# Both SiLUs of a Mamba-2 mixer by ScalarE's own Silu function instead of Tanh and a VectorE product, with the exponentials in the other function table

## The reference, cut to what matters

```
proj = hidden_states @ in_proj_w.T
gate, xBC, dt = jnp.split(proj, [INTER, INTER + CONV_DIM], axis=-1)
conv = causal depthwise convolution of xBC, 4 taps, + conv_b
xBC = jax.nn.silu(conv)                      # first SiLU
x, Bm, Cm = jnp.split(xBC, ...)
y = _ssd(x, Bm, Cm, D, dt, dt_bias)          # scores * exp(decay), two chunks of 128
yg = y * jax.nn.silu(gate)                   # second SiLU
rstd = rsqrt(mean(square(yg)) + EPS) for each of 8 groups
out = (yg * rstd) * norm_w @ out_proj_w.T
```

## Time and profile before

| | |
|---|---|
| median of 3 runs | 1625.1 us (1624.51 to 1627.74) |
| the profiled execution's own time | 1627.01 us |
| its span in the trace | 1625.2 us |
| TensorE busy | 1564.3 us, 96% |
| VectorE busy | 1228.0 us, 76% |
| GpSimd busy | 1052.0 us, 65% |
| ScalarE busy | 1002.3 us, 62% |
| one full mixer group (16 steps and the tail) | 182.5 us |

### The profile page before, as it was taken

One profiled execution on the slowest core, in us unless ns is written; L12 is line 12 of the kernel. 1 busy time (PEld: TensorE's weight loads), 2 busy tenths in 40 slices (PEclk: granted clock), 3 DMA queues, 4 the chain that ended last, 5 costly groups with the idle time before them and its releaser, 6 DMA issues. The chain is left out here.

```text
span 1625.2 us, 25474 instructions
## 1 busy us (share of the span) xinstructions
PE 1564.3 (96%) x8296; PEld 1226.0 (75%) x8296; DVE 1228.0 (76%) x1689; ACT 1002.3 (62%) x2122; POOL 1052.0 (65%) x790
## 2 busy tenths in 40 slices
PE   6979999999999999999999999999999999999979
PEld 4657777777777777777777777777777777777757
DVE  6688877787778877887688877887688877887565
ACT  4357765666666665666666665666666665666431
POOL 2017874788757874788657874787657874787620
PEclk9899999999999999999999999999999999999989
DMA  3033321323222221222212321223222221322011
GB/s 118 1 103 103 107 91 59 92 91 92 78 72 92 92 92 59 91 92 92 78 72 92 92 91 59 92 92 92 78 75 88 92 92 59 98 86 84 20 40 53
DMA packets 73658, 131.65 MB, mean 81 GB/s; under 512 B 10944, under 2 KB 10944, under 8 KB 73280
## 3 DMA queue, kind: packets, MB, share of 16 engines
q1 hardware_dynamic: 73536, 130.09, 24.3%
HBM read 127.44 MB, written 2.62 MB: 80 GB/s over the span
## 5 line engine op out<-in xcount | busy, mean ns | idle before, releaser
L892 DVE SCALAR_TENSOR_TENSOR mx_acc<-bank,mx_cw,mx_acc 128x510 f32<-128x510 f32 (+2 forms) x480 | 358.3, 746 | 160.8 <-ACT mx_acc L877 149.5
L159 PE MATMUL bank<-h_hi,mx_w_hi 128*128 128x512 f32 x1152 | 465.6, 404 | 4.4 <-DVE mx_acc L892 2.3
L161 PE MATMUL bank<-h_hi,mx_w_lo 128*128 128x512 f32 x1152 | 453.1, 393 | 0.0
L160 PE MATMUL bank<-h_lo,mx_w_hi 128*128 128x512 f32 x1152 | 450.2, 391 | 0.0
L1108 ACT ACTIVATE mx_mix<-mx_csb,mx_gncs 128x256 f32<-128x256 f32 x512 | 218.9, 499 | 284.3 <-PE bank L1478 281.3
L1033 POOL TENSOR_TENSOR mx_y<-mx_y,mx_sg 128x512 f32<-128x512 f32 x128 | 338.4, 2644 | 59.7 <-DVE mx_y L1280 51.7
L839 POOL TENSOR_TENSOR mx_w_lo<-mx_w_raw,mx_w_hi 128x512 fp32r<-128x512 f32 x144 | 187.4, 1302 | 111.0 <-ACT mx_w_hi L834 111.0
L161 PEld LDWEIGHTS bank<-h_hi,mx_w_lo 128*128 128x128 f32 x1152 | 216.9, 188 | 48.5
L159 PEld LDWEIGHTS bank<-h_hi,mx_w_hi 128*128 128x128 f32 x1152 | 217.3, 189 | 47.8 <-issue 6.5
L160 PEld LDWEIGHTS bank<-h_lo,mx_w_hi 128*128 128x128 f32 x1152 | 217.7, 189 | 41.5
L1262 DVE TENSOR_TENSOR mx_mix<-mx_mix,mx_cbt 128x1536 f32<-128x1536 f32 x128 | 224.5, 1754 | 0.0
(11 more groups left out here) (163 smaller groups left out, 2203.7 us busy)
## 6 DMA issues: line engine op xcount, KB each, us to landing
mx_csb<-cs_rows SPq DMA_DIRECT2D x128, 512.0 KB, 4.0
mx_w_raw<-in_w_in SPq DMA_DIRECT2D x144, 256.0 KB, 4.0
mx_wo_raw<-in_w_out SPq DMA_DIRECT2D x64, 256.0 KB, 4.2
res<-in_x SPq DMA_DIRECT2D x8, 256.0 KB, 5.0
f_base_raw<-in_base_wt SPq DMA_DIRECT2D x2, 1024.0 KB, 6.1
out<-res SPq DMA_DIRECT2D x8, 256.0 KB, 2.0
f_a_raw<-in_lora_a SPq DMA_DIRECT2D x2, 256.0 KB, 3.8
f_lb_raw<-in_lora_b SPq DMA_DIRECT2D x2, 256.0 KB, 6.2
```

The costliest lines, as they stand in the source:

```text
L159: nc.tensor.matmul(out, w_hi, x_hi, start=first, stop=False)
L160: nc.tensor.matmul(out, w_hi, x_lo, start=False, stop=False)
L161: return nc.tensor.matmul(out, w_lo, x_hi, start=False, stop=last)
L892: self.nc.vector.scalar_tensor_tensor(dst, src[:, :, 0:SEQ - k], self.cw[:, c, TAPS - 1 - k:TAPS - k], dst, ALU.mult, ALU.add).then_inc(s[ ...
```

## The change

ScalarE's `Silu` takes the place of Tanh and of the VectorE product, for the gate (from PSUM into `sg`) and for the convolution (in place in `acc`). VectorE's `silu_gate` and `silu_conv` go, with the buffer `th`. The semaphores `conv` and `sg`, which TensorE and GpSimd wait for, are now raised by ScalarE. The factors 0.5 in the small constant tables become copies. In the step, `square` and `round_tile` move from before `decay_from_second` to the step's end, so that the Exps stand together and everything between the first Silu and the next step's first Exp can use Silu's table.

```
-            def tanh_conv(g, u):
+            def silu_conv(g, u):
                 act.wait_ge(s["tap"], 1 + (TAPS - 1) * (UNITS * g + u + 1))
-                act.wait_ge(s["conv"], 1 + UNITS * g + max(u - 1, 0))
-                nc.scalar.activation(th[:, u % 2, :], acc[:, u % 4, :, :].rearrange("p b t -> p (b t)"),
-                                     ACT.Tanh).then_inc(s["th"], 1)
+                a = acc[:, u % 4, :, :].rearrange("p b t -> p (b t)")
+                nc.scalar.activation(a, a, ACT.Silu).then_inc(s["conv"], 1)
...
-            def tanh_gate(g, st):
+            def silu_gate(g, st):
                 act.wait_ge(s["gate"], 1 + STEPS * g + st + 1)
                 act.wait_ge(s["yg"], 1 + STEPS * g + max(st - 1, 0))
-                nc.scalar.activation(sg[:, st % 2, :], G_BANK[:, :], ACT.Tanh, scale=0.5).then_inc(s["tg"], 1)
+                nc.scalar.activation(sg[:, st % 2, :], G_BANK[:, :], ACT.Silu).then_inc(s["sg"], 1)
...
                     if here or more:
                         evacuate(gn, un)
+                    if here or more:
+                        decay_from_second(gn, stn)
+                    silu_gate(g, st)
+                    if here or more:
+                        silu_conv(gn, un)
+                    if st % 2 == 0:
+                        split_wo(g, st // 2)
+                    if here and has_tile(g, st + 1):
+                        round_tile(g, st + 1)
                     if st >= 1:
                         square(g, st - 1)
-                    if here and has_tile(g, st + 1):
-                        round_tile(g, st + 1)
-                    if here or more:
-                        decay_from_second(gn, stn)
-                    tanh_gate(g, st)
-                    if here or more:
-                        tanh_conv(gn, un)
-                    if st % 2 == 0:
-                        split_wo(g, st // 2)
...
-            def silu_conv(g, u):
-
-                dve.wait_ge(s["th"], 1 + UNITS * g + u + 1)
-                a = acc[:, u % 4, :, :].rearrange("p b t -> p (b t)")
-                nc.vector.scalar_tensor_tensor(a, th[:, u % 2, :], 1.0, a, ALU.add, ALU.mult).then_inc(s["conv"], 1)
...
-            def silu_gate(g, st):
-                dve.wait_ge(s["tg"], 1 + STEPS * g + st + 1)
-                a = sg[:, st % 2, :]
-                nc.vector.scalar_tensor_tensor(a, a, 1.0, G_BANK[:, :], ALU.add, ALU.mult).then_inc(s["sg"], 1)
```

More of the change, by code:

```diff
@@ L801, in __init__ @@
             "const_in", "nw_in", "const", "proj", "gate", "xt", "y", "cb", "out", "ss",
-            "evac", "th", "tg", "decay", "sq", "yhi", "whi", "wohi", "gcopy", "root",
+            "evac", "decay", "sq", "yhi", "whi", "wohi", "gcopy", "root",
             "tap", "conv", "mix", "xd", "sg", "ysb", "cbt", "gsum", "outsb", "ms", "inv", "wolo",
@@ L860, in conv_constants @@
         dve.wait_ge(s["tap"], 1 + (TAPS - 1) * UNITS * g)
-        nc.vector.tensor_scalar(self.cw[:, :, :], self.cw_raw[:, :, :], 0.5, None, ALU.mult).then_inc(s["const"], 1)
-        nc.vector.tensor_scalar(self.cb[:, :], self.cb_raw[:, :], 0.5, None, ALU.mult).then_inc(s["const"], 1)
+        nc.vector.tensor_copy(self.cw[:, :, :], self.cw_raw[:, :, :]).then_inc(s["const"], 1)
+        nc.vector.tensor_copy(self.cb[:, :], self.cb_raw[:, :]).then_inc(s["const"], 1)
         dve.wait_ge(s["const"], 1 + 5 * g + 2)
@@ L919, in mixer_phase @@
         csb = sb("csb", [P, 2, 2, HALF])
-        th = sb("th", [P, 2, HALF])
         xd = sb("xd", [P, 2, HB * 2, 2, HD])
@@ L1079, in _ @@
         def _(act):
-            start_at_one(act, [s["th"], s["tg"], s["decay"], s["sq"], s["wohi"], s["gcopy"], s["root"]])
+            start_at_one(act, [s["conv"], s["sg"], s["decay"], s["sq"], s["wohi"], s["gcopy"], s["root"]])
             start_after_quad(act, [s["yhi"]])
@@ L1154, in _ @@
             act.wait_ge(s["const"], 1 + 3)
-            tanh_conv(0, 0)
-            tanh_conv(0, 1)
+            silu_conv(0, 0)
+            silu_conv(0, 1)
             evacuate(0, 2)
@@ L1159, in _ @@
             evacuate(0, 3)
-            tanh_conv(0, 2)
+            silu_conv(0, 2)
             decay_from_second(0, 0)
             ip.round_w(act, 0, 3)
-            tanh_conv(0, 3)
+            silu_conv(0, 3)
             evacuate(0, 4)
-            tanh_conv(0, 4)
+            silu_conv(0, 4)
             def steps(g, more):
@@ L1202, in tail @@
                     ip.round_w(act, g + 1, 2)
-                    tanh_conv(g + 1, 1)
+                    silu_conv(g + 1, 1)
                     evacuate(g + 1, 2)
                     evacuate(g + 1, 3)
-                    tanh_conv(g + 1, 2)
-                    tanh_conv(g + 1, 3)
+                    silu_conv(g + 1, 2)
+                    silu_conv(g + 1, 3)
                     evacuate(g + 1, 4)
                     ip.round_w(act, g + 1, 3)
-                    tanh_conv(g + 1, 4)
+                    silu_conv(g + 1, 4)
                     root(g)
@@ L1232, in _ @@
         def _(dve):
-            start_at_one(dve, [s["conv"], s["mix"], s["xd"], s["sg"], s["ysb"], s["cbt"],
+            start_at_one(dve, [s["mix"], s["xd"], s["ysb"], s["cbt"],
                                s["ms"], s["inv"], s["wolo"]])
@@ L1327, in head_constants @@
                 dve.wait_ge(s["ysb"], 1 + STEPS * g)
-                nc.vector.tensor_scalar(dh[:, :], d_raw[:, :], 0.5, None, ALU.mult).then_inc(s["const"], 1)
-                nc.vector.tensor_scalar(gdt[:, :, :], m.dtt[:, :, bass.ds(g * GH, GH)], 0.5, None,
-                                        ALU.mult).then_inc(s["const"], 1)
+                nc.vector.tensor_copy(dh[:, :], d_raw[:, :]).then_inc(s["const"], 1)
+                nc.vector.tensor_copy(gdt[:, :, :], m.dtt[:, :, bass.ds(g * GH, GH)]).then_inc(s["const"], 1)
                 dve.wait_ge(s["const"], 1 + 5 * g + 5)
@@ L1343, in _ @@
             keep_bc(0, 1)
-            silu_conv(0, 4)
             def steps(g, more):
@@ L1356, in steps @@
                         ip.taps(dve, gn, un)
-                    silu_gate(g, st)
-                    if here or more:
-                        silu_conv(gn, un)
                     if st % 2 == 1:
```

8 lines of the change are left out of this document (removed).

## The result

The changed kernel took 1806.7 us (median of 4 runs, 1799.7 to 1814.6), the kernel before 1626.1 (4 runs, 1624.5 to 1627.7). The ratio is 1.111, 95% interval 1.106 to 1.117. The forecast was 1709 us, and its range ended at 1760. So the sign was right and the size was half of what came. The profiled execution is the fastest of the four, with a span of 1797.9 us at a granted clock of 0.976; the other three have 1800.5, 1809.3 and 1812.8 us at 0.973, 0.966 and 0.964.

What follows compares the result with a forecast made beforehand. TensorE, busy 96%, was taken to bound the kernel before, a loop ScalarE, GpSimd, ScalarE after. Group 0's 13.4 plus 7 x 10.1 gave 84 us: 1711 for the profiled execution, 1709 for the median, range 1650 to 1760.

Steps and rivals of the forecast that it cites:

- What GpSimd meets in its new place: GpSimd's later `split_tile`, `sum_squares` and select fall beside VectorE's `make_mix` and stretch: 12.0 us late at step 14.
- the meeting: GpSimd's rows overlapping VectorE's `make_mix` after `y`; 0.9 of each overlap added for a tensor_tensor, half for the select.
- A shorter loop: Rival: the overlap with `make_mix` costs nothing, 3.4 us a group, about 10 in group 0, 1659 us; chance 0.16.
- the ring: Loop of ScalarE's `round_tile`, GpSimd's `split_tile`, `sum_squares` and select, ScalarE's next first Exp: average 10.58 and 11.08 against 10.30 us.
- Two loads a step: ScalarE's table loads, 251 in all: 1.31 us each, about 0.1 more for lost overlap, no drain.
- The Silus take Tanh's places: ScalarE's gate and convolution: Silu costed at Tanh's 0.58 and 0.62 us.
- The moved `round_tile`: ScalarE's `yhi` comes at D (first Exp's start) + 7.01 to 8.13, before 5.1; loop 10.27 to 11.39 us without contention.
- VectorE's two products go: Taking both products from VectorE gains nothing inside a group and 0.4 us for each group, at its beginning.
- Group 0: First group: 2.9 us late from prelude loads, 2.7 in steps 1 to 7, some 7.5 from step 8; together 13.4.
- TensorE busy near 91%: Expected profile after the change: TensorE's busy share near 91%, before 96%.
- Select alone 0.63: Expected profile after the change: GpSimd's select takes 0.63 us where it stands alone, before 1.09 beside VectorE's product.
- Transposes waiting about 1 us for Silu: Expected profile after the change: TensorE's transposes wait for ScalarE's Silu about 1 us a step, most from step 5.

Runs made afterwards that it cites:

- run 4: The changed kernel with `make_mix` reading its second operand from PSUM (another tile's data, so values differ), 1678.0 us.
- run 11: The changed kernel with GpSimd's first select ahead and the gate's Silu ahead of `decay_from_second`, so four table loads a step, 1924.7 us.
- Run 7: The changed kernel with Tanh for both Silus (no table loads in the steps, values differ) and `square` and `round_tile` back in their old place, 1609.4 us.
- runs 1 and 5: The changed kernel with `square` and `round_tile` back before the second Exps, 1645.5 us; the second also with GpSimd's first select ahead, 1644.8 us.
- run 3: The changed kernel with GpSimd's first select of the next but one step ahead of `split_tile` and `sum_squares`, 1628.6 us.
- run 5: The changed kernel with `square` and `round_tile` back before the second Exps and GpSimd's first select ahead of `split_tile` and `sum_squares`, 1644.8 us.

## Why the prediction was half right

The mechanism was the one forecast and the size was not. The step that failed is **"What GpSimd meets in its new place"**. The prediction made the meeting worth 50 us (1709 less the 1659 of "A shorter loop"); it measured 129 (1806.7 less the 1678.0 of run 4). I put `make_mix` 0.6 us behind `y` in all steps and walked 12.0 us of lateness to step 14. In step 2 it does start there (739.75, with `y` at 739.08). In step 3 it starts 1.9 us behind `y` (751.24, with `y` at 749.32): VectorE's queue is itself late, since its taps wait for `evacuate`, which comes only after the first Exp of the late ring. So VectorE stands inside the ring. In run 4, where nothing is stretched, `make_mix` starts about 0.7 us behind `y` again. I had seen that shift under "A shorter loop" and thought that it would shrink the overlap. It fixed it instead: steps 3 to 8 all take 11.9 or 12.1 us, where I had 10.9 to 12.3.

By stretches of the middle group of the table (203.2 us against 182.2; forecast 10 more, measured 21; the six between group 0 and the last average 22.2):
- D3 to D9: +10.2, forecast +6.5. The meeting is locked in.
- D0 to D3: +4.0, forecast none. I had said the ring binds only from step 3. But the first Exp waits for the select from step 1 on (0.71 us at 721.51, 1.83 at 732.17), and `split_tile` (2.80 us at 739.88) and the select (2.15 at 729.99) meet `make_mix` there too. Without the meeting (run 4) 1.1 of the 4.0 are left.
- D9 to D14: +6.5, forecast +5.5. Nearly right.
- D14 to D15: +2.8, forecast none. Here the code has one more wait, for the constants, ahead of the Exp. That Exp's own wait for the select then seems to go to its load, which doesn't start early and lies 0.07 us behind the select's end:

```profile
884.26 0.64 POOL L1020 TENSOR_SCALAR_AFFINE_SELECT mx_csb<-mx_csb 128x512 f32<-128x512 f32 x1
```
```profile
884.97 1.28 ACT L1106 ACT_TABLE_LOAD   x1 [3.14 <-issue]
886.26 1.71 ACT L1106 ACTIVATE mx_mix<-mx_csb,mx_gncs 128x256 f32<-128x256 f32 x4
```

- D15 to D0: -2.5, forecast -1.9 (1.8 of lateness that TensorE doesn't feel, and the ends). Near, but by luck: without the low clock it is -4.1 (group 6), with two spells of it -0.9 (groups 1 and 2).

The other steps:
- *Two loads a step.* 273 loads in the trace, before 22: 251. All take 1283 ns, with no drain, also in a full ScalarE (run 11). Right. The Trainium skill, "ScalarE: Activation LUTs", What ACT_TABLE_LOAD costs, gives 2.66 us for a switch, drain included; these traces disagree, with 1.28 us and 0.01 to 0.02 us to the next row.
- *The Silus take Tanh's places.* Gate 0.597 us, convolution 0.62. Right.
- *The moved `round_tile`.* The ring without the meeting was summed to 10.27, 10.89, 10.77 and 11.39 us. Run 4 shows it bare: 10.38, 10.87, 10.75 and 11.35. Right.
- *"A shorter loop"* priced a kernel without the meeting at 1659; run 4 measured 1678. That sum lacked group 0's size (14.0 us late at group 1's D0, where I had about 10) and the last step's load.
- *VectorE's two products go.* I gave it 0.4 us a group. Run 7 shows 16 us: 8.2 in group 0 (148.4 to 140.2), where VectorE paces the early steps, and 0.9 in each other group. The trace of before had the place (group 0's steps of 8 us), and I priced that place only for ScalarE.
- *Group 0.* Forecast 13.4, though its terms 2.9, 2.7 and 7.5 make 13.1; measured 19.4 at group 1's D0 (302.3 against 282.9).
- *TensorE busy near 91%*: 89%. *Select alone 0.63*: 0.64. *Transposes waiting about 1 us for Silu*: 0.53, 1.58 and 1.73 us in three steps in a row.
- *The clock.* The prediction has no term for it. The stretch from D15 to D0 takes 30.4 us in groups 1 and 2, with two spells of 3.4 us at 0.50 in it, 28.8 in groups 3 to 5 with one, and 27.2 in group 6 with none: 1.6 us for each. Steps late in groups 4 to 7 take 12.7 or 12.8 us instead of 11.4, and each follows such a spell. In group 4 it lies from 1025.5 to 1028.9, right behind 2.2 us of idle time of TensorE; `make_mix` starts 1.6 us later against the first Exp than in group 3 (8.0 us behind it, there 6.3) and meets `split_tile`, 2.71 us at 1038.30, where group 3 has 1.31 at 835.17. Together that is some 21 us of the 173 (an estimate, from the seven group ends and six late steps).

Reconciled: 84, 6 more in group 0, 12.1 more in each of six groups, 10.1 in the last, give 173, which is the difference of the two spans (1797.9 less 1625.2). The 181 us between the medians are 8 more, since the changed kernel's profiled execution is its fastest.

What stays open: the other 52 us of run 4 weren't split by a run of their own between ring, group 0, the late load and the clock. No run held the clock fixed, so what it took of the 129 us is known only from the traces. And why the same idle time is followed by a low clock in one group and not in the next isn't shown: in runs 1 and 5 one or two groups of seven were spared after the same 2.2 us.

## What to carry to other kernels

When an instruction is moved later in one engine's queue, follow what stands behind its receiver in the receiver's queue. Here a rounding moved by 2 to 3 us delayed a select that had nothing to do with it, and moving that select ahead (run 3) gave back 178 of 181 us. If the new ring binds, every engine in it slides, so where two of them meet must be worked out from the new order of waits, not from the old distances. And a table load costs its 1.28 us only where it lies on the path, because ScalarE has no idle time (run 11) or because the load itself can't start early (D14 to D15): the same 251 loads cost 16, 36 or 152 us, depending on what hung behind them. Last, a wait of TensorE can cost more than its own length. Look at the granted clock of a long step before you explain it by the order of instructions.

## What the runs showed of the hardware

- VectorE's multiply of two SBUF operands and the GpSimd rows that meet it here don't run side by side. GpSimd's 1.29 us became 2.81 and 2.80, its select's 0.64 became 2.15; VectorE's 1.75 became 2.21 when GpSimd had begun first. The blocked one ends as if it began at the other's end: `make_mix` ends at 753.45 and `sum_squares` at 754.60, 1.15 us later; at 741.50 and 742.68, 1.18. With one operand from PSUM (run 4) both keep their lone times: `make_mix` takes 1.75 us in all 128 steps and `sum_squares` at most 1.31. The Trainium skill, "SBUF — State Buffer", Who interferes with whom, calls the port pair of the two engines an exclusive lock and not a split of bandwidth; the trace agrees, with these numbers.
- A table load placed by the build takes waits of the activation behind it. With one wait more in the code it seems to have taken the select's as well: in a step inside the group it starts 0.02 us behind the row before (750.85) and its Exp alone waits for the select, at the group's end it starts 0.07 us behind the select (884.97), and 1.3 us that are hidden elsewhere came onto the path. In all seven group ends ScalarE is idle for 3.1 us or more ahead of that load.
- Where TensorE idles more, its rows can take longer: those of one middle group take 180.3 us before (granted clock 1.00), 182.7 in the changed kernel (0.99) and 187.3 in run 11 (0.97). Where a spell of 3.4 us at 0.50 lay, the stretch around it was 1.6 us longer (11.48 us against 9.86 in run 5; 30.4, 28.8 and 27.2 with two, one and none in the changed kernel). In run 5 each followed 2.2 us of idle time; 1.7 us in the same place (run 3) was followed by none.
